# Transposing the normalised tokens on TensorE and VectorE instead of by DMA, in the first stage of an attention and mixture-of-experts layer

## The reference

```python
def attn(x, w_qkv, b_qkv, w_proj, b_proj):         # x: layernormed tokens
    qkv = x @ w_qkv + b_qkv
...
    q = elu(q) + 1.0
    k = elu(k) + 1.0
    kv = einsum('bhnd,bhne->bhde', k, v)            # summed over all tokens
    out = einsum('bhnd,bhde->bhne', q, kv)
    z = 1.0 / (einsum('bhnd,bhd->bhn', q, k.sum(axis=2)) + 1e-08)
    return (out * z[..., None]) @ w_proj + b_proj    # heads joined again

x = x + attn(layernorm(x), ...)
x = x + ffn(layernorm(x), ...)
```

## Time and profile before

| | us |
|---|---|
| timed runs, median of 2 | 7826.12 (7642.72 to 8009.52) |
| the profiled execution | 6984.06 |
| its span, slowest core (core 2) | 6982.5 |
| spans of the eight cores | 6976.4 to 6982.5 |
| TensorE busy in the span | 6162.2 (88%) |
| VectorE busy | 2749.7 (39%) |
| ScalarE busy | 838.9 (12%) |

### The profile page before, as it was taken

One profiled execution on the slowest core, in us unless ns is written; L12 is line 12 of the kernel. 1 busy time (PEld: TensorE's weight loads), 2 busy tenths in 40 slices (PEclk: granted clock), 3 DMA queues, 4 the chain that ended last, 5 costly groups with the idle time before them and its releaser, 6 DMA issues.

```text
span 6982.5 us, 76894 instructions; the slowest of 8 cores (6976.4 to 6982.5 us)
## 1 busy us (share of the span) xinstructions
PE 6162.2 (88%) x28982; PEld 2711.1 (39%) x28982; DVE 2749.7 (39%) x4829; ACT 838.9 (12%) x1390; POOL 165.5 (2%) x202
## 2 busy tenths in 40 slices
PE   4776555699999999999999988999999999999999
PEld 1222222244444444444444433444444444444444
DVE  3444444433333333333333333333333333333334
ACT  1221111111111111111111110111111111111110
POOL 0000000000000000000000000000000000000000
PEclk9998666799999999999999999999999999999999
DMA  5112111322222222222222251222222222222222
GB/s 96 41 38 45 52 55 55 94 37 37 37 37 37 37 37 37 37 37 37 37 37 37 37 122 29 37 37 37 37 37 37 37 37 37 37 37 37 37 37 67
DMA packets 233628, 307.02 MB, mean 44 GB/s; under 512 B 46890, under 2 KB 177962, under 8 KB 233266
## 3 DMA queue, kind: packets, MB, share of 16 engines
q0 software_dynamic: 169120, 209.75, 20.2%
q1 hardware_dynamic: 64146, 92.35, 4.3%
HBM read 469.84 MB, written 33.55 MB: 72 GB/s over the span
## 4 chain that ended last, share of the span: by engine, by line
PE 71%; DVE 12%; issue 8%; ACT 4%; DMA 2%; SPq 1%; DVEq 0%; ACTq 0%; POOL 0%; POOLq 0%
PE p3p L740 25%; PE p3g L735 25%; PE p3o L780 14%; DVE out_acc L795 8%; PE p2pr L532 2%; ACT rt L752 2%; PE p1kv L328 2%; SPq L196 1%; DMA out<-out_acc 1%; PE p1q L385 1%; DMA rws<-router_w 1%; DVE h2T L474 1%; PE p2tr L470 1%; ACT acH L571 1%; ACT xt L574 0%
## 5 line engine op out<-in xcount | busy, mean ns | idle before, releaser
L780 PE MATMUL p3o<-wo_p,t 128*128 128x512 bf16 x8192 | 1853.0, 379 | 288.2 <-DVE out_acc L795 288.2
L735 PE MATMUL p3g<-h2T,wg_p 128*128 128x512 bf16 x8192 | 1936.9, 379 | 0.6 <-DVE sk L659 0.6
L740 PE MATMUL p3p<-h2T,wp_p 128*128 128x512 bf16 x8192 | 1935.5, 379 | 0.0
L762 DVE TENSOR_TENSOR t<-rt,p3p 128x512 bf16<-128x512 f32 x1024 | 704.7, 688 | 3022.0 <-ACT rt L752 3021.8
L795 DVE SCALAR_TENSOR_TENSOR out_acc<-p3o,wsel,out_acc 128x512 f32<-128x512 f32 x2048 | 1481.4, 748 | 444.8 <-PE p3o L780 334.5
L780 PEld LDWEIGHTS p3o<-wo_p,t 128*128 128x128 bf16 x8192 | 783.3, 98 | 1316.3 <-issue 410.6
L752 ACT ACTIVATE rt<-p3g 128x512 f32<-128x512 f32 x1024 | 611.3, 597 | 5009.4 <-PE p3p L740 5009.4
L735 PEld LDWEIGHTS p3g<-h2T,wg_p 128*128 128x128 bf16 x8192 | 801.5, 98 | 968.3 <-issue 2.4
L740 PEld LDWEIGHTS p3p<-h2T,wp_p 128*128 128x128 bf16 x8192 | 801.5, 98 | 967.4 <-issue 1.1
L328 PE MATMUL p1kv<-wqkv_sb,h1T 128*128 128x512 bf16 x1024 | 257.9, 397 | 120.0 <-DMA h1T<-h1b 102.4
L196 POOL DMA_DIRECT2D wg_p<-wg x64 | 56.9, 889 | 5986.9 <-DVE out_acc L795 5340.6
(11 more groups left out here) (113 smaller groups left out, 1156.3 us busy)
## 6 DMA issues: line engine op xcount, KB each, us to landing
wg_p<-wg POOLq DMA_DIRECT2D x64, 1024.0 KB, 10.9
wp_p<-wp POOLq DMA_DIRECT2D x64, 1024.0 KB, 16.9
wo_p<-wo POOLq DMA_DIRECT2D x64, 1024.0 KB, 21.3
xt<-x SPq DMA_DIRECT2D x64, 512.0 KB, 3.8
base_scr<-xt SPq DMA_DIRECT2D x32, 512.0 KB, 2.6
out_acc<-base_scr SPq DMA_DIRECT2D x32, 512.0 KB, 7.2
out<-out_acc SPq DMA_DIRECT2D x32, 512.0 KB, 4.4
wqkv_sb<-w_qkv POOLq DMA_DIRECT2D x1, 6144.0 KB, 43.3
```

The lines of the kernel that those rows point to most:

```text
L735: EM(T, lambda t, b=b, k=k, fsub=fsub, w=w, q=q, it3=it3: t.matmul(p3g[it3 % 2][:], wg_sb[b][:, 512 * k + 128 * fsub:512 * k + 128 * (fsub ...
L740: mmfn = lambda t, b=b, k=k, fsub=fsub, w=w, q=q, it3=it3: t.matmul(p3p[it3 % 2][:], wp_sb[b][:, 512 * k + 128 * fsub:512 * k + 128 * (fsu ...
L762: EM(V, lambda v, qt=qt, fsub=fsub, it3=it3: v.tensor_tensor(t_sb[qt][:, 512 * fsub:512 * (fsub + 1)], rt_sb[it3 % 2][:], p3p[it3 % 2][:], ...
L780: mmfn = lambda t, qt=qt, s4=s4, fsub=fsub, b=b, dmh=dmh: t.matmul(p3o[s4][:], t_sb[qt][:, 512 * fsub + 128 * s4:512 * fsub + 128 * (s4 + 1)],
```

## The change

`p1_tr` no longer issues DMAs. TensorE waits for the block `h1b` and transposes its eight 128 x 128 parts against the identity, in turn into `p1tr0` and `p1tr1`, each raising semaphore `tp`; from the third on it waits until the part two before has been copied. VectorE waits for `tp`, copies each part into its place in `h1T` and raises `tpf`. Whoever waited for the DMAs' semaphores (`stpd`: TensorE ahead of the k and v matmuls, ScalarE before it overwrites `h1b`) now waits for `tpf`. The wait of SyncE for `q` goes: TensorE's transposes stand behind its q matmuls in its own list.

```diff
-    stpd = [SM["tpd"], SM["tpd1"]]
+    stpd = [SM["tpf"], SM["tpf"]]
     tpd_hist = []
+    p1tpf_hist = []
...
     def p1_tr(i):
         sup, s4 = divmod(i, 4)
-        W(SY, SM["h1"], i + 1)
-        if sup >= 1:
-            W(SY, SM["q"], 8 * sup)
+        W(T, SM["h1"], i + 1)
         for j in range(8):
-            dma(SY, h1T[:, 512 * j + 128 * s4:512 * j + 128 * (s4 + 1)],
-                h1b[i % 2][:, 128 * j:128 * (j + 1)], stpd[i % 2], tr=True)
-        tpd_hist.append((i % 2, stpd[i % 2].v))
+            tp = i * 8 + j
+            if tp >= 2:
+                W(T, SM["tpf"], p1tpf_hist[tp - 2])
+            EM(T, lambda t, j=j, tp=tp, i=i: t.transpose(p1tr[tp % 2][:], h1b[i % 2][:, 128 * j:128 * (j + 1)],
+                                                         identb[:]).then_inc(SM["tp"].h, 1))
+            inc(SM["tp"])
+            W(V, SM["tp"])
+            EM(V, lambda v, j=j, tp=tp, s4=s4: v.tensor_copy(
+                h1T[:, 512 * j + 128 * s4:512 * j + 128 * (s4 + 1)],
+                p1tr[tp % 2][:]).then_inc(SM["tpf"].h, 1))
+            p1tpf_hist.append(inc(SM["tpf"]))
+        tpd_hist.append((i % 2, SM["tpf"].v))
```

## The result

The changed kernel is slower: the ratio to the kernel before is 1.0178, with a 95% interval of 1.0155 to 1.0201. The profiled execution took 7109.7 us, the one of before 6984.1: 125.6 us more. Both kernels have executions near their shortest (6986, 7109) and others up to 8100 in which the cores of one or both dies show a lower granted clock, so that the median of a few runs says mostly how many of each were drawn; the ratio is made of the undisturbed ones.

The account below looks back on a forecast made before the run. First stage alone in play, TensorE's long wait being 102.4 us for DMA transposes. Terms 108.5 - 24.9 - 2 + 48 = +129.6, about +130 us, on the 7826 median: 7956 us, range 7680 to 8160.

Parts of the forecast that it names:

- (a): Group of eight transposes and copies, priced from the second stage: 2.78 us from VectorE's release to the matmul.
- (b): Ordinary blocks: matmuls wait for copies behind the statistics, 4.64 us in 22 blocks, 3.2 in the last two; +108.5 us.
- (c): Seven blocks opening a group of four: matmul starts at 448.55 instead of 452.10, 3.55 us gained each; -24.9 us.
- (d): Start: block 0's copies stand behind block 2's statistics, matmul at 69.1 against 71.00; -2 us, bounds 9 gained to 0.
- The reserve that the forecast made here for the weights: At the start: gain of 0 if the weights hold TensorE as long as before.
- (e): TensorE's clock falls in the new gap of 24 ordinary blocks, 2.0 us restart each; +48 us, bounds 0 to 68.
- The rule on transposes: Trainium skill's rule that transposes do not count as TensorE being busy for its clock; by it every ordinary block drops.
- the row from the second stage: TensorE worked 0.28 us in 4.10 us, nearly all two transposes; clock fell, then stayed at 0.50 over 6.1 us.
- Rival 1: Clock holds in ordinary blocks, so the sum without the 48 is +82 us, 7908 us; chance 0.17.
- Rival 3: Faster: ordinary blocks' copies ahead of statistics, transposes paced by copies alone, clock held; -18 us, 7808 us; chance 0.1.
- The larger chance, 0.56: Measured effect within 2% of no change; beside it slower by over 2% 0.38, faster by over 2% 0.06.

Follow-up runs that it names:

- the kernel with that half alone: TensorE transposes and VectorE copies in the seven opening blocks only, DMA transposes in the others, against the kernel before: span 6959.9 us, 22.6 less.
- the last runs: Last of them: two h1T buffers, later statistics, block 0 transposed by TensorE with one copy; shortest executions 6895.2 and 6895.7 us, beside 6985.2 and 6985.3 before.
- the fill with matmuls: Changed kernel plus ten unread 512-column matmuls in TensorE's waits between the transposes of each ordinary block: span 7064.5 us, 43.4 less than the changed kernel.
- the fill with transposes: Changed kernel plus thirty unread 128 x 128 transposes in TensorE's waits in each ordinary block: span 7078.8 us, 29.1 less than the changed kernel.
- the run with the later statistics: DMA transposes, two h1T buffers, opening blocks' statistics put behind the second k result: span 6906.2 us, 20.8 less than two buffers alone; ratio to before 0.9891.

## Why the prediction was right in its steps and wrong in its number

The time, 7956 us with a range of 7680 to 8160, missed the measured median of 7522. The step that failed is the base of the sum: "7826 + 130". I took the median of two runs as the level to which the effect is added, although the profiled execution stood 842 us below it and I had no row that explained the difference. With ten runs the same kernel's median was 7619. The low end was widened by only 128 us for this (from 7808, the point of the lowest rival, to 7680), although the two runs lay 659 and 1026 us above the trace on which every term rested. Against the profiled execution the same sum gave 7114 us; the changed kernel's profiled execution took 7109.7. The relative forecast, 1.7% slower, stands beside a measured 1.78%, but part of that closeness is luck: the base was too high and the sum 4 us too large, and on the profiled level the same 130 us are 1.86%. Why the medians of the two kernels lie 633 and 413 us above their shortest executions stays open.

Step by step:

(a) and (b), the gap of an ordinary block, 2.78 us behind the statistics and 4.64 us in all: confirmed, the first to the hundredth (452.42 to 455.20), the second within a tenth (450.55 to 455.20). The last two gaps, without statistics ahead, were 3.2 and 3.0 us, where 3.2 stood. The price from the second stage carried over because shapes, buffers and wait pattern were the same.

(c), -24.9 us: 3.5 us per opening block, -22.6 us in the kernel with that half alone. Right.

(d), -2 us: the first k matmul starts at 68.28 instead of 71.00, -2.7. Right; the last runs showed that what held the start was the order in VectorE's queue and the DMA transposes, since the first k matmul can start at 57. The reserve that the forecast made here for the weights had no ground: in the trace of before, the qkv weights were issued at 3.2 us and had landed 43.3 us later.

(e), +48 us: the fill with matmuls returned 43.4 us with the clock held in 23 of 24 blocks. Right in size. The rule on transposes that stood beside it was too strong, as the fill with transposes showed; the row from the second stage alone would have done.

One reading beside the steps was loose. The 1.25 us that the forecast set beside the Trainium skill's price of a DMA transpose is the distance of two issues in the queue; from issue to landing one transpose took 2.33 us. No term of the sum rests on it.

The sum, +129.6, against +125.4 in the span. The mean period of the 24 blocks with no q behind them rose from 11.56 to 17.46 us (+141.6 in all), that of the seven with q fell from 41.51 to 39.53 (-13.9), the start gave -2.7: 125.0.

Rival 1 (the clock holds) falls by the profile. Rival 3 named the two conditions under which the change would not lose, copies first and a pace set by the copies; the run with one copy, ahead of the statistics, met both in its own way (one copy instead of eight) and came out level with before, 9 us below, with a gap of 1.7 us, under its point of 2.75. The larger chance, 0.56, stood on within 2%, where the measured 1.78% lies; its interval ends at 2.01%, so slower by over 2% is not quite excluded.

## What to carry to other kernels

A wait that is long in a few blocks is not a price per block: before replacing a transfer, look whether the blocks that do not wait had it for nothing, and remove the reason for the wait (here a single buffer) where it arises. When a stall goes, list what other engines did under it; that work is the next wait, here 39 of 94 us. And look how full the queue is that you keep: here it had some 0.3 us to spare per block. If a transpose must go through PSUM, write all parts to one bank and copy once: here it gave back 82 of 125 us.

A gap of a few microseconds on TensorE costs more than itself when the clock falls in it: here 4.64 us of gap and 2.0 of restart. And take the level from the execution whose rows make the sum, not from the median of two runs that the trace does not explain.

## What I had not expected of the hardware

A bf16 copy from PSUM of 128x1024 took 0.69 us, as long as the 128x512 results of f32 in this kernel (0.69 us, L351, L356); eight copies of 128x128 took 0.36 us a pair, 1.44 us in all. The ordinary blocks lost the full clock at gaps as short as 1.7 us: in 10 of 24 with one copy ahead of the statistics, in 13 with gaps of 2.8 us, and in all with gaps of 3.1 us. Thirty extra transposes kept TensorE's clock up in 16 of 24 gaps, and 32 tiny matmuls in 2.36 us did not keep it up ahead of block 13 of the run with the later statistics. The eight DMA transposes of block 0, beside the loading of the first experts' weights (the last landed at 68.4 us), took 10.4 us to issue, hardly more than the 10.0 in the middle of the stage, but the last one took 6.38 us to land instead of 2.33.
